# A two-layer state-space and mixture-of-experts kernel: gate products dealt out one a slot, and the first layer's blocks taken out a slot later

## The chip, the core and the metric

The kernel runs on one core of a Trainium2 chip. The core has a matrix engine (PE, with its weight loads listed as PEld), a vector engine (DVE), an activation engine (ACT), a general engine (POOL) and a queue processor for transfers (SP). Each runs its own list of instructions in order; they wait for each other through semaphores. The metric is the device time of one execution in microseconds (us). Before the change the median of three executions is 685.33 us (684.86 to 688.0).

## The reference

Two layers, each of the form x + s(norm(x)) * silu(f(norm(x))), on 8 sequences of 256 tokens with 128 features. s is a state-space scan, f a mixture of experts. Cut to what matters here:

```python
# layer 0, experts: one expert per token
h = relu(einsum('te,td,edf->tf', onehot, xn, W1) + b1[idx])
y = (einsum('te,tf,efd->td', onehot, h, W2) + b2[idx]) * gates
# layer 1, experts: all 8 experts for every token, F = 512
g = einsum('bsh,ehf->ebsf', x, w_gate)
u = einsum('bsh,ehf->ebsf', x, w_up)
h = silu(g) * u
expert_out = einsum('ebsf,efh->ebsh', h, w_down)
out = einsum('ebsh,bse->bsh', expert_out, cw)
# both layers, scan over tokens, 16 states per feature
s = s * exp(delta * A) + (delta * x) * B
y = sum over the states of s * C
```

## The kernel before, in words

The 2048 tokens are worked on in 4 pairs of sequences (PAIRS), 512 tokens at a time, so that most tiles are 128 x 512. The program of every engine is written as a walk over slots: 32 slots (UNITS) to a pair, 128 in the first layer and 128 in the second. Tables of slot numbers say what an engine does in which slot, and the text of a slot function says in which order. There is no planner: the numbers are written by hand. A slot is an order and no time; an engine goes on as soon as the semaphores let it.

**The scan** is cut into chunks, one for each state index. In the first layer there are 16 chunks to a pair, one every two slots (CH0), in the second 32, one a slot but for one slot with two (CHUNKS1). For each chunk ACT forms the decay (exp), DVE forms the drive (L899 in the first layer, L922 in the second) and runs the scan (L907, L929), and POOL multiplies the state by C (L1320 or L1324, in the second layer L1275) and adds it to a running sum (L1326, L1277). There are 4 state buffers (RING), so DVE can be at most 4 chunks ahead of POOL; and 6 decay buffers (SIX).

**First layer, experts.** The tokens are sorted by expert into 15 blocks of 256 rows. Block b goes through these steps, whose slots hang on UP_AT (20, 24, ... 64, then 67, 70, 73): POOL starts the load of the expert's weights (load_pack, an indirect DMA, L1226) five slots before; PE transposes the rows (turn_block, two slots before); ACT copies them (turn_in, L1613); PE forms the hidden layer (up_block, L1815); ACT applies relu (L1621); PE multiplies by W2 (down_block, L1827, three slots after); DVE adds the bias and takes the result out of PSUM (take_out, L1005, at TAKE_AT, five slots after); SP stores it (eight slots after). The weights have three buffers, so load_pack(b) waits for the take of block b - 3. In the same slots DVE also forms wl, the low part of the second layer's gate weights (split_low, L743), two operands in SBUF.

**Second layer, experts.** 8 experts with 4 tiles of the hidden layer each make 32 units to a pair, one a slot. Unit u takes: the gate product on PE (gate1, three passes in three instructions, L1911 to L1913, into one of two PSUM banks, HIDS = 2), Silu on ACT (L1676, into one of six buffers sg), the up product on PE (up1, L2023, in slot u + 1), the multiplication of the two on DVE (finish_hidden, L1059, in slot u + 2), and the down product on PE (down1, L2041, in slot u + 3). Within a slot PE does its gate products first, then down1, then up1, then the heads of the next pair. ACT runs the 4 Silus of an expert in one burst, since exp and Silu need different tables, and behind them the decays of the chunks that are scanned 3 to 6 slots later. With experts 3 to 6 a head of the next pair ("xi0", "xi1", "z0", "z1" in EXTRA) goes through the same two banks between two experts. POOL also weighs the tokens of expert e + 1 (weigh_tokens, L1384), after the last up product of expert e - 1.

The gate products before: with units 4e to 4e + 3 of expert e, PE does two (one, where EXTRA has a head) in slot 4e - 1, and the other two or three in slot 4e.

Of the kernel before, what the change touches and what calls it, by code (L numbers as in the profile page):

```python
# [37 lines left out]
E, FT = 8, 4  # L38
UNITS = E * FT
# [42 lines left out]


EXTRA = {3: "xi0", 4: "xi1", 5: "z0", 6: "z1"}
PE1 = {6: "xnT", 8: "logits", 9: "xi0a", 10: "xi0b", 13: "row0 xi1a", 15: "cwT xi1b", 17: "dt0", 18: "z0",
       20: "row1", 22: "dt1 z1"}
ACT1 = {5: "xn", 7: "xnT", 10: "lexp", 14: "row0", 15: "cwT", 19: "dt0", 21: "row1", 23: "dt1", 26: "ln", 29: "hand xr",
# [40 lines left out]
SCATTER_AT = [k // 4 for k in range(NT)]  # L128
UP_AT = [20 + 4 * b if b < 12 else 31 + 3 * b for b in range(BLOCKS)]
TURN_AT, TURN_IN_AT = [at - 2 for at in UP_AT], [at - 1 for at in UP_AT]  # L130
RELU_AT, DOWN_AT, TAKE_AT = ([at + lag for at in UP_AT] for lag in (1, 3, 5))
PACK_AT, LOAD_AT = ([at + lag for at in UP_AT] for lag in (-5, -5))
STORE_AT = [at + (8 if b < BLOCKS - 2 else 6) for b, at in enumerate(UP_AT)]
ROWS_AT = 18
# [49 lines left out]
def now(slots, u):  # L184

    if isinstance(slots, dict):
        return slots.get(u, "").split()
    return [c for c, at in enumerate(slots) if at == u]
# [28 lines left out]

STREAM = [item for e in range(E) for item in ([EXTRA[e]] if e in EXTRA else []) + list(range(FT * e, FT * e + FT))]
assert len(STREAM) % HIDS == 0


def stream_bank(item):

    return HID_BANK + STREAM.index(item) % HIDS


def stream_before(item, extras):

    items = [k for k in STREAM if extras or isinstance(k, int)]
    at, bank = STREAM.index(item), stream_bank(item)  # L230
    earlier = [k for k in items if stream_bank(k) == bank and STREAM.index(k) < at]
    return earlier[-1] if earlier else None
# [67 lines left out]
def build(nc, x, out, x1, crow, cwrow, sorted_in, sorted_out, w):  # L300
    ctx = ExitStack()
    with ctx:
# [209 lines left out]
        def use1(signal, j, step):  # L512
            return signal.sem, signal.at1(j, bank_order(j).index(step) + 1)
# [17 lines left out]
        def first_pair(j):  # L531

            return isinstance(j, int) and j == 0
# [915 lines left out]
        def _(act):  # L1449
# [132 lines left out]
            def keep(i):  # L1582

                act.wait_ge(*use1(head_read, i, "xi1"))
                act.wait_ge(s_ps.sem, s_ps.at1(i, 0))
                for m in range(J1):
                    a.activation(xd[:, m, :], xs[:, m, :], ACT.Identity, scale=col1("dskip", m))
                act.wait_ge(*use1(head_read, i, "z1"))
                act.wait_ge(yz_ready.sem, yz_ready.at1(i, 0))
                a.activation(szm[:, :, :], sz[:, :, :], ACT.Copy, scale=0.5).then_inc(kept_ready.sem, 1)  # L1590
# [15 lines left out]
            def form_decay(i, c):  # L1606
                exponential(in1(i), c, c // N, negA1, freed(c, i))
# [64 lines left out]
            def silu(i, u):  # L1672
                act.wait_ge(hid_ps.sem, hid_ps.at1(i, u + 1))

                act.wait_ge(hid_ready.sem, hid_ready.at1(i, freed(u, i)))
                a.activation(sg[:, PLACE[u], :], bank[stream_bank(u)][:, :], ACT.Silu).then_inc(silu_ready.sem, 1)  # L1676

            def slot1(i, u, head=None, j=None, late=None):
                e = u // FT
                if u == 0 and late is first_late:  # L1680
                    act.wait_ge(g_ready.sem, g_ready.at0(PAIRS, 0))
                if u == 0 and late:
                    late(u)
                if u % FT == 0:
                    if e in EXTRA and i + 1 < PAIRS:
                        head1({"x": "xs", "z": "sz"}[EXTRA[e][0]] + EXTRA[e][-1], i + 1)
                    for f in range(FT):
                        silu(i, u + f)
                    if u > 0 and late:
                        late(u)  # L1690
                    for c in DECAYS1[e]:
                        form_decay(i, c)
                elif late:
                    late(u)
                if u == (LATE if i else FIRST_LATE):
                    keep(i)
                if i + 1 < PAIRS:
                    for name in now(ACT1, u):
                        head1(name, i + 1)
# [40 lines left out]
            for u in range(FIRST_LATE):  # L1740
                slot1(0, u, late=first_late)
            for i in range(PAIRS - 1):
                for u in range(LATE if i else FIRST_LATE, UNITS):
                    slot1(i, u, head1, i + 1)
                for u in range(LATE):
                    slot1(i + 1, u, late=lambda u: late1(i, u))
# [7 lines left out]
        def _(pe):  # L1754
# [75 lines left out]
            def head_free(j, name):  # L1830

                order = bank_order(j)
                earlier = order[:order.index(name)]
                if first_pair(j):
                    same = [k for k in earlier if BANK_OF10[k] == BANK_OF10[name]]
                else:
                    same = [k for k in earlier if k not in EXTRA.values()]
                pe.wait_ge(head_read.sem, head_read.at1(j, order.index(same[-1]) + 1 if same else 0))

            def extra_free(j, name):  # L1840

                if first_pair(j):
                    head_free(j, name)
                    if BANK_OF10[name] == OUT_BANK:
                        pe.wait_ge(blk_out_ready.sem, blk_out_ready.at0(0, BLOCKS))
                    return
                before = stream_before(name, True)
                pe.wait_ge(silu_ready.sem, silu_ready.at1(j - 1, before + 1))
# [11 lines left out]
            def head1(name, j):  # L1860
# [3 lines left out]
                if name in ("xi0", "xi1", "xi0a", "xi1a", "z0", "z1"):  # L1864
                    extra_free(j, item)
                elif item not in EXTRA.values():
                    head_free(j, name)
# [41 lines left out]
            def three_passes(dst, e, f, stop):  # L1909
                ws = slice(128 * f, 128 * f + 128)  # L1910
                t.matmul(dst, wh[:, e, ws], XH[:, :], start=True, stop=False)  # L1911
                t.matmul(dst, wh[:, e, ws], XL[:, :], start=False, stop=False)  # L1912
                return t.matmul(dst, wl[:, e, ws], XH[:, :], start=False, stop=stop)  # L1913
# [30 lines left out]
            def gate1(i, u):  # L1944
                e, f = u // FT, u % FT
                if u == 0:
                    pe.wait_ge(xl_ready.sem, xl_ready.at1(i, 1))
                    if first_pair(i):
                        pe.wait_ge(*use1(head_read, 0, "cwT"))
                if f == 0:  # L1950
                    pe.wait_ge(wl_ready.sem, wl_ready.at0(0, e + 1))

                before = stream_before(u, i + 1 < PAIRS)
                if before is None:
                    pe.wait_ge(silu_ready.sem, silu_ready.at1(i, u + 1 - HIDS))
                elif isinstance(before, int):
                    pe.wait_ge(silu_ready.sem, silu_ready.at1(i, before + 1))
                else:
                    pe.wait_ge(*use1(head_read, i + 1, before))
                three_passes(bank[stream_bank(u)][:, :], e, f, True).then_inc(hid_ps.sem, 1)  # L1960
# [83 lines left out]
            def slot1(i, u, head=None, j=None, late=None):  # L2044
                if u == 0 and late:
                    late(u)
                more = i + 1 < PAIRS
                if u % FT == 0:
                    for k in range(1 if more and u // FT in EXTRA else 2, FT):
                        gate1(i, u + k)  # L2050
                if u % FT == FT - 1 and u + 1 < UNITS:
                    for k in range(1 if more and (u + 1) // FT in EXTRA else 2):
                        gate1(i, u + 1 + k)
                if u > LAG1:
                    down1(i, u - LAG1)
                if u > 0 and late and u <= LAG1:
                    late(u)
                if u == LAG1:
                    down1(i, u - LAG1)
                if u > 0:  # L2060
                    up1(i, u - 1)
                if late and u > LAG1:
                    late(u)
                if u == UNITS - 1 and more:
                    gate1(i + 1, 0)
                    gate1(i + 1, 1)
                if i + 1 < PAIRS:
                    for name in now(PE1, u):
                        head1(name, i + 1)
                else:  # L2070
                    for n in now(LAST_SUM_AT, u):
                        sum_last(n)
# [38 lines left out]
            for u in range(FIRST_LATE):  # L2111
                slot1(0, u, late=lambda u: late0(PAIRS - 1, u))
# [88 lines left out]
```

## Time and profile before

| what | value |
|---|---|
| median of three executions | 685.33 us |
| the profiled execution, its own time | 684.94 us |
| its span, first to last instruction | 683.2 us |
| DVE busy | 585.9 us (86%) |
| PE busy | 576.1 us (84%) |
| POOL busy | 533.4 us (78%) |
| ACT busy | 451.9 us (66%) |
| mean granted clock of PE | 0.962 |
| first scan of the first layer starts | 41.0 us |
| first scan of the second layer starts | 255.5 us |
| last scan starts | 667.9 us |

Busy time is what the records of an engine cover; matmuls are pipelined and their ends modelled, so starts are the better measure on PE. "Idle before" is how long an engine stood still ahead of an instruction, and the name behind the arrow is what it was waiting for. Lines of matmuls with x2 are one fp32 product recorded in two parts. The 1.7 us between the span and the time lie around the first and the last instruction.

### The profile page before, as it was taken

The numbers are of one execution on the slowest core, as the hardware profiler recorded it, in microseconds if no ns is written. First come the engines' busy times: TensorE is split into PE (matmuls) and PEld (weight loads), VectorE is DVE, ScalarE is ACT, GpSimd is POOL, SyncE is SP. The second block draws the span as 40 slices with busy tenths as digits, with TensorE's granted clock in tenths as the row PEclk, the third lists the DMA queues.
The fourth block names the chain that finished last, engine by engine and source line by source line (L and its number), as shares of the span: only waits on it lengthen the run. The fifth ranks groups of instructions, "written<-read, shape, count | busy, mean of one in ns | idle before, by whom it ended". The sixth has DMA issues, their size and how long they took to land. (4 is left out here: it accounts for less than half of the span.)

```text
span 683.2 us, 8361 instructions
## 1 busy us (share of the span) xinstructions
PE 576.1 (84%) x2075; PEld 331.4 (49%) x2075; DVE 585.9 (86%) x921; ACT 451.9 (66%) x708; POOL 533.4 (78%) x431
## 2 busy tenths in 40 slices
PE   3646998889638957999999799999799999799997
PEld 2411676667214423644444454444354444566674
DVE  6899887879898979997879988988989788898995
ACT  4555676866724768757786766787665887766660
POOL 3456568665884577987998899999799999799991
PEclk9998999999877989999999999999999999999999
DMA  8087988997888677776667678657676867787970
GB/s 264 23 309 229 321 315 260 305 342 234 269 266 282 200 175 182 193 199 164 168 165 204 169 192 209 184 158 201 170 198 181 214 164 184 182 213 202 231 190 17
DMA packets 71216, 142.25 MB, mean 208 GB/s; under 512 B 8352, under 2 KB 37088, under 8 KB 71168
## 3 DMA queue, kind: packets, MB, share of 16 engines
q1 hardware_dynamic: 67984, 130.74, 68.1%
q0 software_dynamic: 3184, 10.98, 4.7%
q8 instruction: 17, 0.28, 0.2%
q14 instruction: 31, 0.25, 0.1%
HBM read 133.23 MB, written 8.45 MB: 207 GB/s over the span
## 5 line engine op out<-in xcount | busy, mean ns | idle before, releaser
L929 DVE TENSOR_TENSOR_SCAN state<-decay,bank 128x512 f32<-128x512 f32 x128 | 155.9, 1218 | 13.4 <-POOL product L1275 5.4
L2023 PE MATMUL bank<-xw,wu 128*128 128x512 f32 x256 | 133.0, 601 | 13.7 <-DVE hid L1059 13.5
L1275 POOL TENSOR_TENSOR product<-state,CB 128x512 f32<-128x512 f32 x90 | 116.8, 1297 | 17.7 <-DVE state L929 13.9
L1277 POOL TENSOR_TENSOR product<-product 128x512 f32<-128x512 f32 x90 | 119.8, 1332 | 7.1
L1676 ACT ACTIVATE sg<-bank 128x512 f32<-128x512 f32 x128 | 75.4, 597 | 65.7 <-PE bank L1913 56.9
L2041 PE MATMUL bank<-hid,wd 128*128 128x512 f32 x192 | 99.1, 597 | 6.0 <-DVE hid L1059 6.0
L1059 DVE TENSOR_TENSOR hid<-sg,bank 128x512 f32<-128x512 f32 x128 | 84.9, 665 | 21.8 <-PE bank L2023 20.2
L1925 PE MATMUL bank<-product,early 128*128 128x512 f32 x112 | 71.7, 739 | 33.6 <-POOL product L1320 14.6
L922 DVE TENSOR_TENSOR bank<-bank,CB 128x512 f32<-128x512 f32 x128 | 88.8, 694 | 12.8 <-DMA CB<-crow 10.9
L1596 ACT ACTIVATE decay<-delta,negA 128x510 f32<-128x510 f32 x128 | 82.5, 710 | 10.7 <-DVE delta L887 5.4
L1911 PE MATMUL bank<-XH,wh 128*128 128x512 f32 x128 | 73.5, 574 | 10.5 <-ACT sg L1676 3.7
L907 DVE TENSOR_TENSOR_SCAN state<-decay,bank 128x512 f32<-128x512 f32 x64 | 77.9, 1216 | 2.8
L2023 PEld LDWEIGHTS bank<-xw,wu 128*128 128x128 f32 x256 | 45.4, 191 | 63.7 <-issue 46.5
L1320 POOL TENSOR_TENSOR product<-state,CB 128x512 f32<-128x512 f32 x31 | 40.5, 1305 | 23.6 <-DVE state L907 16.6
L1604 ACT ACTIVATE decay<-delta,negA 128x510 f32<-128x510 f32 x64 | 44.9, 714 | 16.5 <-DVE state L907 16.3
L1925 PEld LDWEIGHTS bank<-product,early 128*128 128x128 f32 x112 | 22.4, 229 | 64.5 <-POOL product L1320 27.4
L2041 PEld LDWEIGHTS bank<-hid,wd 128*128 128x128 f32 x192 | 35.1, 189 | 34.5 <-issue 25.9
L1913 PE MATMUL bank<-XH,wl 128*128 128x512 f32 x128 | 50.6, 395 | 0.0
L1912 PE MATMUL bank<-XL,wh 128*128 128x512 f32 x128 | 50.5, 395 | 0.0
L1911 PEld LDWEIGHTS bank<-XH,wh 128*128 128x128 f32 x128 | 24.4, 190 | 39.3 <-ACT sg L1676 13.3
L1596 ACT ACT_TABLE_LOAD x32 | 41.1, 1283 | 0.6
L1384 POOL TENSOR_TENSOR xw<-XR,cwb 128x512 f32<-128x512 f32 x30 | 39.4, 1312 | 2.4 <-PE bank L2023 1.0
(240 smaller groups left out, 1117.7 us busy)
## 6 DMA issues: line engine op xcount, KB each, us to landing
CB<-crow SPq DMA_DIRECT2D x256, 256.0 KB, 4.1
CB<-crow SPq DMA_DIRECT2D x44, 512.0 KB, 5.0
cwb<-cwrow SPq DMA_DIRECT2D x32, 256.0 KB, 4.6
szm<-crow SPq DMA_DIRECT2D x11, 512.0 KB, 5.3
cwb<-crow SPq DMA_DIRECT2D x9, 512.0 KB, 5.6
xw<-Wg_dram SPq DMA_DIRECT2D x8, 256.0 KB, 4.5
wd<-Wd_dram SPq DMA_DIRECT2D x8, 256.0 KB, 5.7
wu<-Wu_dram SPq DMA_DIRECT2D x8, 256.0 KB, 4.7
```

Of the source, the lines that this page charges most:

```text
L907: v.tensor_tensor_scan(state[:, g % RING, :], place0(g), drive, 0.0, ALU.mult, ALU.add).then_inc(state_ready.sem, 1)
L922: v.tensor_tensor(drive, dx, CB[:, c % ROWS, 1, :], ALU.mult).then_inc(drive_ready.sem, 1)
L929: v.tensor_tensor_scan(state[:, c % RING, :], decay[:, PLACE[c], :], drive, 0.0, ALU.mult, ALU.add).then_inc(state_ready.sem, 1)
L1059: v.tensor_tensor(hid[:, u % 2, :], sg[:, PLACE[u], :], bank[up_bank(i, u)][:, :], ALU.mult).then_inc(hid_ready.sem, 1)
L1275: p.tensor_tensor(addend, state[:, c % RING, :], cs, ALU.mult).then_inc(state_used.sem, 1)
L1277: ins = p.tensor_tensor(product[:, m, :], product[:, m, :], addend, ALU.add)
L1596: a.activation(by_batch(decay[:, PLACE[c], :])[:, :, 1:], by_batch(delta[:, m, :])[:, :, 1:], ACT.Exp, scale=negA[:, c:c + 1]).then_inc(de ...
L1676: a.activation(sg[:, PLACE[u], :], bank[stream_bank(u)][:, :], ACT.Silu).then_inc(silu_ready.sem, 1)
L1911: t.matmul(dst, wh[:, e, ws], XH[:, :], start=True, stop=False)
L1925: t.matmul(bank[Y_BANK][:, :], ident[:, :], product[:, PRODUCT_OF[n], :], start=(c == 0), stop=(group[-1] % N == N - 1)).then_inc(summed.s ...
L2023: t.matmul(bank[up_bank(i, u)][:, :], wu[:, e, 128 * f:128 * f + 128], xw[:, e % 2, :], start=True, stop=True).then_inc(up_ps.sem, 1)
L2041: ins = t.matmul(bank[OUT_BANK][:, :], wd[:, u, :], hid[:, u % 2, :], start=(u == 0), stop=(u == UNITS - 1))
```

## The change

Three edits. (1) The order of the gate products in the second layer comes from two tables instead of the two if-statements. In pairs with a next pair (GATE1_AT): expert 0 as before but for unit 3 in slot 1 (nothing lies between there); expert 1 as before (3, 3, 4, 4); experts 2 and 7 one a slot (6 to 9, and 26 to 29); experts 3 to 6 in slots 4e - 1, 4e, 4e, 4e + 1. In the last pair (GATE1_LAST) every expert but 1 has one a slot. (2) ACT's Silus of an expert other than 1 are written as two in slot 4e and two in slot 4e + 1, with the decays behind the second two. (3) take_out of blocks 0 to 10 stands six slots after up_block instead of five.

```diff
+GATE1_LAST = [-1, -1] + [k // FT * FT + (-1, -1, 0, 0)[k % FT] if k // FT == 1 else k - 2 for k in range(2, UNITS)]
+GATE1_AT = [k // FT * FT + (-1, 0, 0, 1)[k % FT] if k // FT in EXTRA else at for k, at in enumerate(GATE1_LAST)]
...
-RELU_AT, DOWN_AT, TAKE_AT = ([at + lag for at in UP_AT] for lag in (1, 3, 5))
+RELU_AT, DOWN_AT = ([at + lag for at in UP_AT] for lag in (1, 3))
+TAKE_AT = [at + (6 if b < 11 else 5) for b, at in enumerate(UP_AT)]
...
-                    for f in range(FT):
+                    for f in range(FT if e == 1 else 2):
                         silu(i, u + f)
                     if u > 0 and late:
                         late(u)
+                elif u % FT == 1 and e != 1:
+                    for f in range(2):
+                        silu(i, u + 1 + f)
+                    if late:
+                        late(u)
+                elif late:
+                    late(u)
+                if u % FT == (0 if e == 1 else 1):
                     for c in DECAYS1[e]:
                         form_decay(i, c)
-                elif late:
-                    late(u)
...
-                if u % FT == 0:
-                    for k in range(1 if more and u // FT in EXTRA else 2, FT):
-                        gate1(i, u + k)
-                if u % FT == FT - 1 and u + 1 < UNITS:
-                    for k in range(1 if more and (u + 1) // FT in EXTRA else 2):
-                        gate1(i, u + 1 + k)
+                for k in now(GATE1_AT if more else GATE1_LAST, u):
+                    gate1(i, k)
```

PE, first pair of the second layer, slots 16 and 17 (expert 4, units 17 to 19). L1911 to L1913 are one gate product (L1920 to L1922 after, the lines having moved by nine), `hid,wd` is down1, `xw,wu` is up1. Before:

```order
L1911 MATMUL bank2<-XH,wh 128x512
L1912 MATMUL bank2<-XL,wh 128x512
L1913 MATMUL bank2<-XH,wl 128x512
L1911 MATMUL bank3<-XH,wh 128x512
L1912 MATMUL bank3<-XL,wh 128x512
L1913 MATMUL bank3<-XH,wl 128x512
L2041 MATMUL bank1<-hid,wd 128x512
L2023 MATMUL bank5<-xw,wu 128x512
L2041 MATMUL bank1<-hid,wd 128x512
L2023 MATMUL bank0<-xw,wu 128x512
```

After:

```order
L1920 MATMUL bank2<-XH,wh 128x512
L1921 MATMUL bank2<-XL,wh 128x512
L1922 MATMUL bank2<-XH,wl 128x512
L2050 MATMUL bank1<-hid,wd 128x512
L2032 MATMUL bank5<-xw,wu 128x512
L1920 MATMUL bank3<-XH,wh 128x512
L1921 MATMUL bank3<-XL,wh 128x512
L1922 MATMUL bank3<-XH,wl 128x512
L2050 MATMUL bank1<-hid,wd 128x512
L2032 MATMUL bank0<-xw,wu 128x512
```

The gate product of unit 19 has moved from ahead of slot 16's down and up product to behind them. The same happens with the fourth unit of experts 2 to 7 in every pair; with experts 2 and 7 (in the last pair with experts 2 to 7) the first unit also moves a slot ahead.

DVE, first layer, block 8, slots 57 and 58. `hid<-bank1,wd` is take_out, `bank4<-bank6` the drive of a chunk, `state<-decay,bank4` its scan, `wl<-xw,wh` split_low. Before:

```order
L899 TENSOR_TENSOR bank4<-bank6,cwb 128x512
L907 SCALAR_TENSOR_TENSOR state<-decay,bank4 128x512
L1005 TENSOR_TENSOR hid<-bank1,wd 128x256
L899 TENSOR_TENSOR bank4<-bank6,szm 128x512
L743 TENSOR_TENSOR wl<-xw,wh 128x512
L907 SCALAR_TENSOR_TENSOR state<-decay,bank4 128x512
```

After:

```order
L902 TENSOR_TENSOR bank4<-bank6,cwb 128x512
L910 SCALAR_TENSOR_TENSOR state<-decay,bank4 128x512
L902 TENSOR_TENSOR bank4<-bank6,szm 128x512
L1008 TENSOR_TENSOR hid<-bank1,wd 128x256
L746 TENSOR_TENSOR wl<-xw,wh 128x512
L910 SCALAR_TENSOR_TENSOR state<-decay,bank4 128x512
```

The take of the block now comes behind the next chunk's drive instead of ahead of it. With blocks 3, 4, 6 and 7 it also passes one or two operations of a head.

On ACT, POOL and SP every row is the same before and after: in slots 4e of all experts but the second there is nothing that ACT does between the second and the third Silu, so writing the burst in two halves changes no order.

## Rows read from the trace of the kernel before

**Rows 1.** stretches: start:end, length, busy PE, PEld, DVE, ACT, POOL, clock, DMA, GB/s.
```profile
85.00:170.00 85.00, 76.56 (x410) 58.55 (x409) 69.54 (x106) 59.87 (x120) 56.29 (x46) 0.96 0.86 292
295.00:325.00 30.00, 29.05 (x83) 14.25 (x81) 25.23 (x36) 20.62 (x30) 24.32 (x20) 1.00 0.69 180
365.00:390.00 25.00, 20.43 (x75) 11.48 (x74) 22.73 (x37) 20.02 (x30) 20.80 (x18) 1.00 0.67 170
```

**Rows 2.** waits of POOL, 255 to 683 us: total us, times, longest us.
```profile
POOL product L1275 <- DVE state L929: 13.9, 12, 2.2
```

**Rows 3.** timeline of POOL, second layer: start, us, engine, line, operation, idle before.
```profile
314.07 1.29 POOL L1275 TENSOR_TENSOR product<-state,CB 128x512 f32<-128x512 f32 x1 [0.94 <-DVE state L929]
...
317.73 1.30 POOL L1384 TENSOR_TENSOR xw<-XR,cwb 128x512 f32<-128x512 f32 x1 [1.02 <-PE bank L2023]
320.28 1.28 POOL L1275 TENSOR_TENSOR product<-state,CB 128x512 f32<-128x512 f32 x1 [1.25 <-DVE state L929]
...
383.19 1.28 POOL L1275 TENSOR_TENSOR product<-state,CB 128x512 f32<-128x512 f32 x1 [1.90 <-DVE state L929]
...
427.67 1.28 POOL L1275 TENSOR_TENSOR product<-state,CB 128x512 f32<-128x512 f32 x1 [0.34 <-DVE state L929]
```

**Rows 4.** timeline of DVE, first pair of the second layer, slots 17 to 19.
```profile
317.59 0.69 DVE L1059 TENSOR_TENSOR hid<-sg,bank 128x512 f32<-128x512 f32 x1 [3.60 <-PE bank L2023]
...
318.98 1.22 DVE L929 TENSOR_TENSOR_SCAN state<-decay,bank 128x512 f32<-128x512 f32 x1
...
321.48 1.22 DVE L929 TENSOR_TENSOR_SCAN state<-decay,bank 128x512 f32<-128x512 f32 x1
```

**Rows 5.** timeline of PE, the same stretch, its slot 16.
```profile
314.47 0.40 PE L1913 MATMUL bank<-XH,wl 128*128 128x512 f32 x1
314.87 0.50 PE L1911 MATMUL bank<-XH,wh 128*128 128x512 f32 x1
...
315.67 1.02 PE L2041 MATMUL bank<-hid,wd 128*128 128x512 f32 x2
316.53 1.02 PE L2023 MATMUL bank<-xw,wu 128*128 128x512 f32 x2
```

**Rows 6.** timeline of ACT, the same expert: its last Silu and its decays.
```profile
315.87 0.60 ACT L1676 ACTIVATE sg<-bank 128x512 f32<-128x512 f32 x1 [0.37 <-PE bank L1913]
...
317.78 2.55 ACT L1596 ACTIVATE decay<-delta,negA 128x510 f32<-128x510 f32 x4
```

**Rows 7.** waits of DVE in the first layer, 40 to 250 us.
```profile
DVE hid L1005 <- PE bank L1827: 12.5, 8, 3.6
```

**Rows 8.** timeline of DVE in the first layer.
```profile
93.93 0.75 DVE L846 SCALAR_TENSOR_TENSOR sp_e<-xpad,early,sp_e 128x512 f32<-128x512 f32 x1 [1.17 <-ACT sp_e L1481]
...
119.03 0.42 DVE L1005 TENSOR_TENSOR hid<-bank,wd 128x256 f32<-128x256 f32 x1 [3.64 <-PE bank L1827]
...
119.98 0.69 DVE L899 TENSOR_TENSOR bank<-bank,CB 128x512 f32<-128x512 f32 x1
120.58 1.38 DVE L743 TENSOR_TENSOR wl<-xw,wh 128x512 fp32r<-128x512 f32 x1
...
132.73 0.42 DVE L1005 TENSOR_TENSOR hid<-bank,wd 128x256 f32<-128x256 f32 x1 [2.53 <-PE bank L1827]
```

**Rows 9.** timeline of PE in the first layer.
```profile
86.61 1.95 PE L1827 MATMUL bank<-wd,sg 128*128 128x128 f32 x16
88.73 1.96 PE L1815 MATMUL bank<-sg,wd 128*128 128x256 f32 x8 [0.18 <-issue]
...
126.14 3.29 PE L1815 MATMUL bank<-sg,wd 128*128 128x256 f32 x8 [2.44 <-ACT sg L1613]
...
138.32 1.96 PE L1815 MATMUL bank<-sg,wd 128*128 128x256 f32 x8 [0.91 <-issue]
```

**Rows 10.** DMA issues by tensor: count and median us to landing.
```profile
wd<-pack_dram,rows_of POOLq DMA_INDIRECT x15, 7.0
```

**Rows 11.** the line that forms wl: ns min/median/max of one, first and last start.
```profile
L743 DVE TENSOR_TENSOR wl<-xw,wh x8: 678/681/1379, 89.5 to 186.6; 128x512 fp32r<-128x512 f32 x8
```

## The prediction

> **What bounds the kernel now.** I read the busy times by stretch first, then the waits of POOL and DVE, and then the timelines where these waits lie.
>
> In the first layer's block stretch (85 to 170 us) PE is busy 76.6 of 85 us and DVE 69.5, at a granted clock of 0.96 [rows 1]. Neither runs through: DVE hands states to POOL, POOL issues the weights of a block, PE multiplies, DVE takes the block out. The reader is to see a ring of engines here, and a wait in it tells nothing until one knows what the engine behind it was waiting for.
>
> In the second layer the engine to watch is POOL. Of its idle time 13.9 us, in 12 waits, are waits for a scan ahead of L1275 [rows 2]. The timeline says where: in the first pair (0.94, 1.02 and 1.25 us), a single 0.34 us in the second, and at the start of every pair, as the 1.90 us at 383.19 [rows 3]. The last kind lies where DVE is busy 22.7 of 25 us (third of [rows 1]): DVE is late there by its own work, and no edit touches that. Nearly everywhere else POOL runs without a gap, and a DVE that comes earlier only fills the four state buffers.
>
> **The second layer, part by part.** No product is added or removed; three gate products per expert move. What matters is what they stand ahead of. In slot 16 of the first pair DVE stands 3.60 us for the up product of unit 15, the longest wait of that layer [rows 4], because PE does three gate products before it. The third begins when its predecessor ends (314.47 + 0.40 = 314.87) and the down product behind it starts at 315.67, so it takes 0.80 us [rows 5]. Behind the up product, it frees that product 0.80 us earlier. DVE's multiplication goes from 317.59 to 316.8, the scan of 318.98 to 318.2, and POOL's weighing of 317.73, which waited for the same product, to 316.9. POOL's next product, at 320.28, follows the scan, also 0.80 earlier. So 1.02 + 1.25 us of idle time fall by 0.80 and not to nothing, for PE is busy 29.05 of 30 us here (second of [rows 1]): it has as much to do as before, and what leaves slot 16 stands ahead of the next up product. Bounds: 0 if that next product takes it all back, 2.27 if both waits go. I take 0.80.
>
> In the second pair the same wait of DVE costs POOL 0.34 (last of [rows 3]): I take it whole, from 0 to 0.34. In the third and fourth pair expert 4 leaves no gap on POOL: 0. In experts 5 to 7 of all pairs DVE waits less or not for PE and POOL is busy throughout: 0; the cover is POOL's queue of states, and if it were gone a moved gate would be worth its 0.80 there too. The gate of unit 8, which moves ahead into slot 6, falls in the part where DVE is the late one and PE waits for it: 0. Sum for the second layer: 0.80 + 0.34 = 1.14 us.
>
> ACT's Silus in two halves: its order does not change, so no table load and no operation is added, 0. What changes is the wait of the last Silu for a gate that comes later. Before, it starts at 315.87 and the decays at 317.78, 0.64 each (2.55 for four) [rows 6]; the first of them is used by the scan of slot 19, at 321.48 [rows 4], which leaves 321.48 - 318.42 = 3.06 us. The gate now comes behind a down and an up product, whose starts lie 0.86 apart [rows 5], so 1.72 later, and the scan comes 0.80 earlier: 0.54 us remain. Hidden, narrowly, by DVE's own operations between two scans. If the cover is gone the scan waits for its decay: the first rival on the slow side.
>
> **The first layer.** take_out of blocks 0 to 10 moves behind the next drive. DVE waits 12.5 us in 8 places for PE's down product at this line [rows 7], two of them 3.64 and 2.53 us [rows 8]. The drive, which starts 0.60 us before its follower (119.98 to 120.58) [rows 8], now runs inside the wait. So where DVE waits it gets ahead by 0.60 us, once. It can't be added up over the blocks if PE doesn't come earlier: the next take then waits longer by the same 0.60. Is PE itself waiting for DVE? Three cases show in its rows. Early, PE is back to back: the down product of 86.61 lasts to 88.56 and the up product starts at 88.73, with 0.18 idle [rows 9]; the block before it has the same picture. In the middle the up product of 126.14 waited 2.44 us for ACT [rows 9], whose queue DVE's take doesn't reach; the lead is lost there. Late, 0.91 us before 138.32 [rows 9], named "issue". PE waits for no engine there, and the weights of that block come by a DMA that needs 7.0 us to land [rows 10]; POOL issues it behind the product of a state which DVE delivers. That one comes earlier when DVE is earlier. I count the two early ones with 0.18 each, 0.36, rounded up to 0.4 for DVE's next wait, for ACT at 93.93 (1.17 us) [rows 8], which goes back to PE as well; and the late one with the 0.60 of the lead, as the next load is tied to the scan and not to the gap. Sum 1.0 us. Bounds: 0, if ACT's chain at 126 us and the loads eat all; 4.2, if each of six waiting takes gives back 0.60 and the one at 119.03 a further 0.60 for the head's operation it also passes. I take 1.0, since the rows of PE speak for a ring with little slack.
>
> For blocks that did not wait the take is the same 0.42 us [rows 8] a step later: 0. POOL's load of block b + 3 waits for the take. It stands behind the product of a state that DVE scans in the same stretch, so it is ready as before except for blocks 12 and 13, whose loads wait one DVE step more (0.42 + 0.69); POOL has only work behind it that needs the scan after that. The store on SP has two slots left instead of three: 0.
>
> One place where the Trainium skill speaks against the edit. split_low (wl) takes 0.68 us as a rule and 1.38 once, at 120.58 [rows 8, 11]. The page "SBUF — State Buffer", section "Who interferes with whom", says that a DVE instruction with two SBUF inputs and a GpSimd instruction that reads SBUF shut each other out for a whole instruction. The trace agrees with that one row of eight. By that rule, moved steps may meet POOL's operations anew, and the sum would shrink.
>
> Sum: 1.14 + 1.0 = 2.14 us. The profiled execution took 684.94 us, 0.39 less than the median 685.33; from the median the forecast is 683.2, and I give 683.1 for the small waits of PE for Silus, which the dealing out removes and which I did not count.
>
> **The rivals.**
> A. The first layer keeps every removed wait: 4.2 instead of 1.0, in all 5.3 us, 680.0. For it: the waits are real idle time of a DVE that is busy 82% there. Against: PE at 90% in the same stretch and the wait for ACT at 126.14.
> B. The second layer's first pair loses all of POOL's idle time around expert 4: 0.94 + 1.02 + 1.25 + 0.34 = 3.55, with the first layer's 1.0 in all 4.55 us, 680.8. For it: PE's order is smoother in every slot, and DVE's shorter waits at 307 to 312 us may help too. Against: PE's 97% there.
> C. Slower: the decays come late. Its place is the scan in slot 4e + 3 of experts 2 to 7, it decides from 0.54 us of further delay of the last Silu. Were half of the 24 places uncovered and late by 0.5 us each, that is 6 us against 2.1 gained: 689.2. For it: 0.54 is little, and ACT has a table load before the decays. Against: the Silu waits for the same PE whose up product DVE needs as well, so the two are late together.
> D. DVE's moved steps meet POOL: three more of wl's kind of collision, 0.70 each (1.38 - 0.68), take 2.1 us back: 685.2. For it: the row at 120.58. Against: it can as well remove that one.
>
> **How the numbers follow.** Forecast 0.40, A 0.22, B 0.14, C 0.10, D 0.14. A measurement of this kernel tells about 0.5% (3.4 us) from no change. Faster by more: A, B and 0.05 of the forecast, 0.41. Within: 0.35 of the forecast and 0.13 of D, 0.48. Slower: C and 0.01 of D, 0.11. The range takes in A, B, D and the near side of C: 679.0 to 686.8. The likeliest case's own range is 681.0 to 684.9.
>
> **What would show it.** In the profile after, around 317 us: DVE's wait for the up product shrinks from 3.60 by 0.8 (A says the same, B by 2 and more), and POOL's 1.02 nearly goes. The first scan of the second layer, at 255.5 us before, starts near 254.5; at 251.3 A is right. DVE's waits at L1005 fall from 12.5 to 9 us or less, without the layer getting shorter by as much. Decays before L929 show no wait for ACT; if they do in many places, C. The last scan, at 667.9, should start near 665.8. The forecast is wrong if the layers' two parts don't come to 1 us each, above all if PE's gaps ahead of L1815 stay and the first layer is still shorter.

## The result, and the profile after

Slower. The median is 691.0 us (685.1 to 696.17, 20 runs) against 686.07 (683.38 to 688.0, 20 runs) for the kernel before in the same measurement. The ratio is 1.0071, with a 95% interval of 1.0046 to 1.0096. The forecast was 683.1 us and the range ended at 686.8.

The profiled execution has a span of 690.3 us, 7.1 more than before. It took 692.09 us, 1.1 more than the median, so the profiles show a larger difference than the 4.9 us between the medians. Where it went is read from the starts of the scans: the first scan of the second layer (chunk 0) starts at 255.59 us, before at 255.46, where I had forecast 254.5. So the first layer is even in these two profiles. From there to the last scan it takes 419.5 us (675.08 - 255.59), before 412.5 (667.93 - 255.46). Nearly all of the 7.1 us lie in the second layer, where I had forecast 1.14 us of gain.

The stretches of [rows 1], after (start:end, length, busy PE, PEld, DVE, ACT, POOL, clock, DMA, GB/s):

```profile
85.00:170.00 85.00, 76.95 (x413) 59.76 (x412) 69.60 (x103) 60.97 (x122) 54.80 (x45) 0.96 0.87 290
295.00:325.00 30.00, 28.89 (x82) 14.20 (x80) 26.23 (x37) 20.02 (x29) 25.44 (x21) 1.00 0.70 186
365.00:390.00 25.00, 21.95 (x78) 12.33 (x77) 23.62 (x39) 19.66 (x30) 20.59 (x17) 1.00 0.61 160
```

None of them shows the loss: the stretches I had chosen are not those where it happens. The waits do, for the second layer (total us, times, longest). First POOL's, then PE's, then DVE's:

```profile
POOL product L1278 <- DVE state L932: 23.0, 15, 2.9
```

```profile
PE bank L1920 <- ACT sg L1679: 7.4, 6, 2.3
PE bank L1773 <- ACT rows L1565: 5.1, 3, 1.7
```

```profile
DVE hid L1062 <- PE bank L2032: 31.7, 18, 4.5
```

POOL's wait for scans grew from 13.9 us [rows 2] to 23.0. DVE's wait for up products grew from 20.2 to 31.7. And PE now waits for ACT: 5.1 us for a copy named `rows`, a wait that the kernel before does not have in this layer, and 7.4 us for Silus, before 1.7. The reader should see a chain here, which the experiments below test: ACT late, hence PE, hence DVE, hence POOL.

**At expert 4 the step went as forecast at first.** The mixed timeline of the kernel after around 316 us (start, us, engine, line, operation, idle before):

```profile
315.17 1.02 PE L2032 MATMUL bank<-xw,wu 128*128 128x512 f32 x2
315.63 0.80 PE L1920 MATMUL bank<-XH,wh 128*128 128x512 f32 x1
...
316.23 0.69 DVE L1062 TENSOR_TENSOR hid<-sg,bank 128x512 f32<-128x512 f32 x1 [2.36 <-PE bank L2032]
...
316.65 1.30 POOL L1387 TENSOR_TENSOR xw<-XR,cwb 128x512 f32<-128x512 f32 x1
...
316.73 1.02 PE L2050 MATMUL bank<-hid,wd 128*128 128x512 f32 x2
...
317.61 1.22 DVE L932 TENSOR_TENSOR_SCAN state<-decay,bank 128x512 f32<-128x512 f32 x1
...
318.91 1.28 POOL L1278 TENSOR_TENSOR product<-state,CB 128x512 f32<-128x512 f32 x1 [0.96 <-DVE state L932]
```

DVE's 3.60 us [rows 4] are 2.36, the scan has moved from 318.98 to 317.61, and POOL's 1.02 [rows 3] is gone. The gain is 1.25 us (the scan before this one was 0.12 us ahead already). But the scan of chunk 22 starts at 331.82, before at 331.78: the lead is gone within one expert, and before PE stands still for anything that is told below. 0.41 us of it went in one DVE operation of the next pair's head (L859, 1.45 us at 330.45, before 1.04 at 330.81), the rest by longer waits for PE's up products.

The page of the profile puts a mean of 676 ns on L1920, before 574 on L1911, as if a gate product cost more between other products. The starts say otherwise. From the up product at 315.17 to the down product at 316.73 it is 1.56 us; 0.86 of it is the distance of two such products, and 0.70 is left for the gate product between them, where the kernel before spends 0.80.

**At expert 5 the loss begins.** Before, around 333 us:

```profile
327.89 0.60 ACT L1676 ACTIVATE sg<-bank 128x512 f32<-128x512 f32 x1 [0.36 <-PE bank L1913]
328.51 1.28 ACT L1596 ACT_TABLE_LOAD   x1
...
329.80 2.55 ACT L1596 ACTIVATE decay<-delta,negA 128x510 f32<-128x510 f32 x4
...
332.26 0.58 ACT L1562 ACTIVATE rows<-bank 96x512 f32<-96x512 f32 x1
...
333.79 1.12 PE L1764 MATMUL bank<-rows,w_dt 32*128 32x512 f32 x2
...
334.95 0.69 ACT L1488 ACTIVATE sp_e<-bank,early 128x512 f32<-128x512 f32 x1 [2.11 <-PE bank L1764]
...
337.37 1.02 PE L2023 MATMUL bank<-xw,wu 128*128 128x512 f32 x2
...
338.42 0.69 DVE L1059 TENSOR_TENSOR hid<-sg,bank 128x512 f32<-128x512 f32 x1 [0.44 <-PE bank L2023]
```

After, the same place:

```profile
330.80 0.60 ACT L1679 ACTIVATE sg<-bank 128x512 f32<-128x512 f32 x1 [2.68 <-PE bank L1922]
331.42 1.28 ACT L1599 ACT_TABLE_LOAD   x1
...
332.71 2.55 ACT L1599 ACTIVATE decay<-delta,negA 128x510 f32<-128x510 f32 x4
...
335.17 0.57 ACT L1565 ACTIVATE rows<-bank 96x512 f32<-96x512 f32 x1
...
335.89 1.09 PE L1773 MATMUL bank<-rows,w_dt 32*128 32x512 f32 x2 [1.69 <-ACT rows L1565]
...
339.11 1.91 PE L2050 MATMUL bank<-hid,wd 128*128 128x512 f32 x2
...
340.82 1.28 PE L2032 MATMUL bank<-xw,wu 128*128 128x512 f32 x2
...
342.13 0.69 DVE L1062 TENSOR_TENSOR hid<-sg,bank 128x512 f32<-128x512 f32 x1 [4.11 <-PE bank L2032]
...
345.28 1.27 POOL L1278 TENSOR_TENSOR product<-state,CB 128x512 f32<-128x512 f32 x1 [2.93 <-DVE state L932]
```

The last Silu of the expert is 2.91 us later, since its gate product (unit 23) stands behind a down product, an up product and a product of the next pair's head. Behind that Silu ACT has a table load, four decays and the copy `row1` (`rows`). The decays are in time: no scan waits for one. The copy is not: PE's queue has the product dt1 next, and stands still for 1.69 us. The stretches 335:339, 339:342 and 342:345, before:

```profile
335.00:339.00 4.00, 3.38 (x9) 1.46 (x9) 3.47 (x5) 3.91 (x6) 3.84 (x4) 1.00 0.94 242
339.00:342.00 3.00, 2.49 (x10) 1.76 (x11) 2.44 (x4) 2.14 (x4) 2.84 (x3) 1.00 0.47 139
342.00:345.00 3.00, 3.00 (x9) 1.32 (x8) 1.13 (x2) 2.81 (x4) 2.84 (x3) 1.00 0.54 152
```

and after:

```profile
335.00:339.00 4.00, 3.11 (x7) 1.71 (x8) 2.93 (x4) 2.66 (x6) 3.84 (x4) 0.86 0.39 98
339.00:342.00 3.00, 3.00 (x6) 1.27 (x6) 0.00 (x0) 2.97 (x4) 2.84 (x3) 0.61 0.86 232
342.00:345.00 3.00, 3.00 (x12) 1.82 (x10) 2.87 (x4) 1.20 (x3) 0.35 (x1) 1.00 1.06 243
```

After the standstill the granted clock falls: its mean over 339 to 342 us is 0.61, near the lower of the two levels (1.2 of 2.4 GHz), and the down product takes 1.91 us instead of 1.02. PE is busy 3.00 of 3 us there, and DVE 0.00: a full row of PE is a slow PE. DVE's multiplication is 3.71 us late (342.13 against 338.42, from scans that were even). Of it 2.10 is dt1 (335.89 against 333.79), and 1.61 the rest of the way (1.35 until the up product starts, 0.26 its own length).

Not all of the 3.71 us stay. The scan behind that multiplication (chunk 25) is 3.71 us late too, the next one (chunk 26) only 1.36 (346.62 against 345.26), because the kernel before waits 2.43 us for its next up product there and this one does not wait. In the second and third pair 1.66 and 1.71 us stay at this place. That is 4.7 us of the 7.0 in all; the runs below price this one gate product at 3.9 and 5.5 us.

**At the change from expert 6 to 7** there is a second one. After:

```profile
352.78 1.28 ACT L1679 ACT_TABLE_LOAD   x1
...
354.08 1.09 ACT L1679 ACTIVATE sg<-bank 128x512 f32<-128x512 f32 x2
...
354.73 0.61 PE L1920 MATMUL bank<-XH,wh 128*128 128x512 f32 x1 [2.28 <-ACT sg L1679]
...
355.99 1.91 PE L2050 MATMUL bank<-hid,wd 128*128 128x512 f32 x2
...
359.10 0.69 DVE L1062 TENSOR_TENSOR hid<-sg,bank 128x512 f32<-128x512 f32 x1 [3.77 <-PE bank L2032]
```

Unit 27's gate is late, so expert 6's decays, the head's `ln` with its table loads, and the first Silu of expert 7 are late, and PE waits 2.28 us for the PSUM bank that this Silu frees; before it waited 0.58. From chunk 29 to the first chunk of the next pair 1.43, 0.31 and 0.34 us are added in the three pairs, 2.1 us in all; the first is the pair whose granted clock falls behind the wait:

```profile
355.00:359.00 4.00, 4.00 (x8) 1.98 (x8) 0.33 (x1) 0.76 (x2) 3.76 (x4) 0.58 0.78 204
```

In the first layer DVE's waits at the take fell, as the prediction wanted, from 12.5 us [rows 7] to 7.3. The profile of `warm_dt1` below, with the same first layer, has 10.5, so one profile says little here.

### The profile page after: what moved, and what is told of

Same layout as the page of the kernel before. It is cut to its first block and busy times, and to the rows that moved or that the text cites. A ratio compares the mean times of both kernels' runs of the same rounds, so it can differ in the third digit from the quotient of the medians.

```text
span 690.3 us, 8361 instructions
## 1 busy us (share of the span) xinstructions
PE 579.1 (84%) x2075; PEld 335.9 (49%) x2075; DVE 588.7 (85%) x921; ACT 450.6 (65%) x708; POOL 531.9 (77%) x431
## 5 line engine op out<-in xcount | busy, mean ns | idle before, releaser
L1062 DVE TENSOR_TENSOR hid<-sg,bank 128x512 f32<-128x512 f32 x128 | 85.2, 667 | 33.8 <-PE bank L2032 31.7
L2050 PE MATMUL bank<-hid,wd 128*128 128x512 f32 x192 | 101.2, 609 | 2.8 <-DVE hid L1062 2.8
L1920 PE MATMUL bank<-XH,wh 128*128 128x512 f32 x128 | 86.6, 676 | 16.0 <-ACT sg L1679 9.3
L1922 PE MATMUL bank<-XH,wl 128*128 128x512 f32 x128 | 51.7, 404 | 0.0
L1920 PEld LDWEIGHTS bank<-XH,wh 128*128 128x128 f32 x128 | 24.8, 194 | 49.2 <-issue 17.9
```

Source lines behind the costliest of these rows:

```text
L1062: v.tensor_tensor(hid[:, u % 2, :], sg[:, PLACE[u], :], bank[up_bank(i, u)][:, :], ALU.mult).then_inc(hid_ready.sem, 1)
L2050: ins = t.matmul(bank[OUT_BANK][:, :], wd[:, u, :], hid[:, u % 2, :], start=(u == 0), stop=(u == UNITS - 1))
```

## The experiments

Ratios are to the kernel before on the same chip, each with its 95% interval. "Unit 23 back" means that its gate product stands in slot 20 again, "unit 27 back" in slot 24, in the first three pairs.

**1. The two halves of the change apart.** `take_only`: the kernel before with

```diff
-RELU_AT, DOWN_AT, TAKE_AT = ([at + lag for at in UP_AT] for lag in (1, 3, 5))
+RELU_AT, DOWN_AT = ([at + lag for at in UP_AT] for lag in (1, 3))
+TAKE_AT = [at + (6 if b < 11 else 5) for b, at in enumerate(UP_AT)]
```

> Only take_out of blocks 0 to 10 a slot later, the second layer as before. Theory H (ACT hands over late: the loss is all in the second layer): the first scan of the second layer starts within 0.3 us of 255.5 us and the time is that of before, ratio 0.999 to 1.001. Rival T (the take's move costs, for down_block b + 1 now waits for it behind a head's operation, 1.99 us at 108.5 in the changed kernel's trace): second layer later by 0.5 us or more, ratio above 1.001. My prediction had it 1.0 us earlier, ratio 0.9985.

0.9988 (0.9961 to 1.0015). In its profile the first scan of the second layer starts at 252.53 us, 2.9 earlier than before, which neither H nor T had; part 6 shows how far such starts spread. `gates_only` is the changed kernel with these lines as before.

> Only the gate products dealt out (and the Silus written in two halves), take_out as before. H: the whole loss is here, ratio 1.006 to 1.010, PE waits for ACT's copy of rows ahead of dt1 three times, 1.7 us each, and for ACT's Silu ahead of unit 30's gate, 2.3 us each. T: ratio clearly below the changed kernel's, under 1.004.

1.0104 (1.0060 to 1.0148), with PE's waits for `rows` of 5.1 us and for sg of 7.4, as in the changed kernel. That is just above H's 1.010, with a wide interval. The loss belongs to the gates.

**2. Single gates put back.** `u23_back` is the changed kernel with

```diff
+GATE1_AT[23] = 20
```

> The changed kernel with the gate product of unit 23 (expert 5's fourth) back in slot 20. H: ACT's Silu, decays and copy of rows come 2.7 us earlier, so PE's 5.1 us of waits for rows vanish and the granted clock around 340 us stays at 1.0; the waits ahead of unit 30's gate stay. Time 2 to 4 us under the changed kernel, ratio to before 1.001 to 1.005. Rival O (dealt-out gates cost PE more each, by the changes of weights between them): the time falls by a seventh of the loss only, 1 us.

0.9990 (0.9967 to 1.0014): 0.0081 under the changed kernel, some 5.5 us for three gate products, more than the 2 to 4 us that I expected. The waits for `rows` are gone, the clock of 335 to 345 us is 1.00. `u23_u27_back` has `GATE1_AT[27] = 24` besides:

> Units 23 and 27 (the fourth of experts 5 and 6) back in slots 20 and 24. H: both kinds of PE waits for ACT vanish, what stays is the gain at expert 4: ratio to before 0.996 to 0.999. Rival O: ratio still above 1.003, since 6 of 8 moved gates per pair are still dealt out.

0.9964 (0.9938 to 0.9990), PE's waits for sg down from 7.4 us to 2.3. `u27_back` has unit 27 back alone:

> The changed kernel, with unit 27's gate product (expert 6) back in slot 24; unit 23's stays dealt out. With the kernel that has 23 back (0.999 of before) and the one that has both (0.9964) this completes the square. If the two places add up: 27 is worth 0.0026, so this comes to 1.0045, 2 us under the changed kernel; PE's waits for sg fall from 7.4 to 2.3 us, those for rows stay at 5.1. If instead expert 6's loss is what is left of expert 5's (one is late because the other is), 27 alone is worth nothing: 1.007.

1.0041 (1.0021 to 1.0061), sg 2.3 and `rows` 5.1 us. So the square is additive: unit 23 costs 0.0081 with 27 dealt out and 0.0077 without, unit 27 costs 0.0030 and 0.0026 (the latter two are about as large as their uncertainty, but PE's waits tell the same). `u19_back_too` has units 19, 23 and 27 back:

> The changed kernel with units 19, 23 and 27 back in slots 16, 20 and 24 of the first three pairs: of the dealing out only experts 2 and 7 and the last pair are left, and the takes of the first layer. Beside the kernel that has 23 and 27 back (0.9964) it tells what expert 4's move is worth. If my step for expert 4 was right (DVE's wait of 3.60 at 317 falls by about 0.8 and lasts to the end of the pair once experts 5 and 6 don't lose it): 1 to 2 us slower than that kernel, 0.998 to 1.0. If the lead is lost again at expert 5 whatever is done there: the same as that kernel, 0.996 to 0.997, and the gain comes from the first layer and experts 2 and 7.

0.9983 (0.9962 to 1.0005), against 0.9964 with unit 19 dealt out. The difference, 0.0019 or 1.3 us, is within what the expectation gave the step for expert 4, and the second layer is 412.9 us against 411.7 in the two profiles; but the intervals overlap, so it is not shown.

**3. Unit 23 alone**, in the kernel before:

```diff
-                        gate1(i, u + k)
+                        if not (more and u + k == 23):
+                            gate1(i, u + k)
+                if more and u == 21:
+                    gate1(i, 23)
```

> The kernel before, with one thing changed: unit 23's gate product stands in slot 21 in place of 20, in the first three pairs. Nothing else is dealt out and the first layer is as before. Theory Q (this one move, through ACT's queue, makes most of the loss): the changed kernel with 23 put back was 0.0081 of the time under the changed kernel, so this one comes out as much over the one before: 1.006 to 1.009, PE's wait for ACT rows three times, about 5 us, DVE's wait ahead of the scan of chunk 27 about 4 us each time. If the loss needs the others (late Silus that add up along experts 4 to 6): under 1.004.

1.0057 (1.0037 to 1.0076). Its waits, PE's and then DVE's of the first pair:

```profile
PE bank L1764 <- ACT rows L1562: 5.1, 3, 1.7
```

```profile
341.77 0.69 DVE L1059 TENSOR_TENSOR hid<-sg,bank 128x512 f32<-128x512 f32 x1 [4.51 <-PE bank L2023]
```

One gate product moved by one slot, three times, makes 3.9 us of the 4.9 us. It is a little under what I expected (1.006 to 1.009); the interval takes in both. DVE's wait is 4.5 us in each of the three pairs, ahead of the scan of chunk 25 (the "chunk 27" of the expectation counts two scans of the token sorting with the chunks).

**4. Is it the Silu, or the queue behind it?** `row1_early` is the changed kernel with the copy ahead of the decays; unit 23 stays dealt out.

```diff
+                if u == 21 and i + 1 < PAIRS:
+                    head1("row1", i + 1)
                 if u % FT == (0 if e == 1 else 1):
                     for c in DECAYS1[e]:
                         form_decay(i, c)
...
                     for name in now(ACT1, u):
-                        head1(name, i + 1)
+                        if name != "row1":
+                            head1(name, i + 1)
```

> The changed kernel, with one ACT operation moved: the copy of the next pair's rows (row1) is written ahead of the four decays of expert 5, not behind them; unit 23's gate product stays behind slot 20's down and up product. Theory Q (the late Silu itself costs nothing, ACT's queue behind it does: PE stands 1.7 us per pair ahead of dt1, and its granted clock falls behind that): PE's waits 'L1773 <- ACT rows' (3 times, 5.1 us) go to under 1 us, the granted clock of 335 to 342 us is 0.95 or more instead of 0.61 to 0.86, the second layer gets shorter by 3 to 5 us, time 0.995 of the changed kernel's, 1.001 to 1.004 of the one before. Theory G (a dealt-out gate product costs PE by its place between down and up products, with more weight changes): no change, 1.007, and the gate passes of that stretch stay at 0.6 us.

0.9990 (0.9969 to 1.0010), the same as with unit 23 back and less than the 1.001 to 1.004 expected:

```profile
329.65 0.60 ACT L1679 ACTIVATE sg<-bank 128x512 f32<-128x512 f32 x1 [2.68 <-PE bank L1925]
330.14 0.58 ACT L1565 ACTIVATE rows<-bank 96x512 f32<-96x512 f32 x1
...
332.98 1.12 PE L1776 MATMUL bank<-rows,w_dt 32*128 32x512 f32 x2
...
337.61 0.69 DVE L1062 TENSOR_TENSOR hid<-sg,bank 128x512 f32<-128x512 f32 x1 [0.76 <-PE bank L2035]
```

The Silu waits for PE as long as in the changed kernel (2.68 us), and it costs nothing that these runs can tell. The copy comes 0.49 us behind it and PE doesn't stop. The control is the kernel before with only the copy moved:

> Control: the kernel before, all its gate products in their places, with only ACT's copy row1 of the first three pairs moved ahead of the four decays of expert 5. If row1_early got its 5.4 us back because the late copy was the way in which unit 23's gate hurt, then here, where PE never waits for the copy, there is little to win: 0.998 to 1.002. If the earlier copy is a gain of its own (an earlier load of CB): 0.992 to 0.995, and then row1_early says nothing of unit 23.

1.0002 (0.9985 to 1.0020). An early copy is worth nothing measurable by itself, only where the gate is late. Theory G falls with this pair of runs: the gate product stands where it stood, and the loss is gone.

**5. Standstill or clock?** `warm_dt1` is the changed kernel with PE kept at work during the standstill:

```diff
+                        if name == "dt1":
+                            extra_free(i + 1, "z1")
+                            for _ in range(2):
+                                t.matmul(by_batch(extra_bank(i + 1, "z1")), w_in1[:, 0:128], XNT, start=True, stop=True)
                         head1(name, i + 1)
```

> The changed kernel, with two throwaway fp32 products of 128x512 on PE ahead of dt1 in the first three pairs, 0.86 us each by the starts of such products: as long as the wait of 1.69 us that stands there. Nothing is done earlier; PE only doesn't stand still. Theory W (the larger part of the loss is the lowered clock behind the standstill): the granted clock of 335 to 342 us stays at 0.95 or more, the down product behind takes 1.02 instead of 1.91 us and the gate passes 0.4 instead of 0.6, 1 to 1.5 us a pair back, in all 3 to 4 us, 1.002 to 1.003 of the kernel before. Theory S (the standstill itself is the loss, the clock a bystander): same time as the changed kernel, 1.007, or 0 to 1 us more.

1.0059 (1.0037 to 1.0081): not the 1.0025 of theory W. In the first pair:

```profile
335.69 1.88 PE L2077 MATMUL bank<-XNP,later 128*128 128x512 f32 x4
...
337.54 1.09 PE L1773 MATMUL bank<-rows,w_dt 32*128 32x512 f32 x2
...
340.22 1.02 PE L2050 MATMUL bank<-hid,wd 128*128 128x512 f32 x2
...
342.13 0.69 DVE L1062 TENSOR_TENSOR hid<-sg,bank 128x512 f32<-128x512 f32 x1 [2.47 <-PE bank L2032]
...
345.05 0.70 DVE L925 TENSOR_TENSOR bank<-bank,CB 128x512 f32<-128x512 f32 x1 [2.23 <-DMA CB<-crow]
```

On PE theory W holds: the granted clock of 335 to 345 us is 1.00, the down product takes 1.02, and DVE's wait is 1.64 us shorter, as the 1.61 above says. The end says something else. The next operation, the drive of chunk 25, waits 2.23 us for the load of CB. The data of this load have long been written; what is late is its issue. In SP's queue the program puts the write of `rows` to `crow` just ahead of the load of CB for chunk 25, so SP stands at that write until the late copy is there, and the loads behind it wait too. First this run, then the changed kernel:

```profile
337.42 0.79 SPq L599 DMA_DIRECT2D crow<-rows  x2
338.26 6.62 SPq L592 DMA_DIRECT2D CB<-crow  x8
```

```profile
335.77 0.79 SPq L599 DMA_DIRECT2D crow<-rows  x2
336.60 5.75 SPq L592 DMA_DIRECT2D CB<-crow  x8
```

SP's waits for this copy are 24.2 us in the second layer of the changed kernel, 8.0 at most, and before 11.5 and 3.7. In the changed kernel the late load was hidden behind the slow PE: its drive starts at 342.74 without a wait, 6.14 us behind the first of these loads. Here it starts 6.79 us behind it, so at least 0.65 of the 2.23 us are the load's own spread. In the other two pairs the wait is 0.25 and 0.74 us. Of the 1.6 us the scan of chunk 25 gets 0.5 in those two pairs, and in the first it is 0.7 us later than in the changed kernel. So the clock made the loss at PE longer, but the late copy also holds the pair up by a second way, and what remained of the gain is within the measurement. Theory S, in which the clock is a bystander, is right about the time and wrong about the mechanism.

**6. The first layer's price again, and both repairs.** `u23_u27_back_no_take` has units 23 and 27 back and the takes as before:

> The changed kernel with units 23 and 27 back in slots 20 and 24 and the first layer's takes back at five slots: the gate products of experts 2, 4, 7 and of the last pair alone. With takes at six slots it was 0.9964. It prices the edit of the first layer a third time (two pairs so far: 0.9988 against 1, and 1.0071 against 1.0104). If the takes bring the 1.0 us that I forecast: 0.998. If they bring nothing: 0.9964. If they bring the upper bound of 4.2 us: 1.0025.

0.9986 (0.9962 to 1.0010), against 0.9964 with the new takes. `row1_early_u27_back` has the early copy and unit 27 back:

> The changed kernel with both repairs: unit 27's gate back in slot 24, and the row1 copy ahead of the decays while unit 23 stays dealt out. If the two losses are separate and add up: 1.0071 - 0.0081 - 0.0030 = 0.996, as with both gates put back (0.9964), and PE waits neither for rows (0) nor for more than 2.5 us for sg. If mending one uncovers the other again: 0.999 or more.

0.9952 (0.9935 to 0.9969): 682.64 us (680.59 to 683.79, 9 runs) against 685.82 for the kernel before. The two repairs add up, and this version beats both kernels. Why it is better than before by 3.3 us is not settled by one profile: its second layer has 412.8 us there, the kernel before 412.5, and between profiles of the same code such a length differs by about 1 us (413.3 in `take_only`). In these two profiles the difference lies ahead of the second layer, whose first scan starts at 252.83 us against 255.46.

## Why the prediction was wrong

The step that failed is the price of ACT's late Silus, which the sum put at nothing; it turned a small gain into a loss. The gain at expert 4 also did not last as it was forecast.

- **"ACT's Silus in two halves: 0, hidden, narrowly."** This failed, twice over. The delay was mis-sized: I let the gate pass a down and an up product (1.72 us), but in expert 5 the first product of the next pair's head stands there too, 2.91 us in the trace. And I asked only who uses the decays. They were covered. What wasn't is the next thing in ACT's queue, the copy `row1`, on which PE's own queue hangs and SP's too, with the loads of CB behind it. Its cover can be read in the kernel before: the copy ends at 332.84, and PE gets to dt1 at 333.70 (332.84 + 0.86 for the up product ahead), so 0.86 us. A delay of 2.91 us, less 0.86, less the 0.33 by which PE itself came later, is 1.72; the wait measured is 1.69. Even my own 1.72 us of delay would have overrun it. The 2.11 us that ACT waits at 334.95 in the kernel before look like room, but they lie behind the copy.
- **"In experts 5 to 7: 0; the cover is POOL's queue of states."** I asked what a gain is worth there, not what a loss is. The cover is there, but it is shorter than the loss: POOL's product of chunk 25 starts 1.03 us later than before (345.28, with a wait of 2.93, against 344.25) behind a scan that is 3.71 us late. (By the tables one gate product moves in each of experts 3 to 6 and two in experts 2 and 7, not three per expert as the prediction says; no term of the sum used the three.)
- **Expert 4, +0.80 and +0.34.** Direction and place right. The up product comes 1.36 us earlier (315.17 against 316.53); 0.40 of it PE was ahead at the first gate of the slot (312.82 against 313.22), 0.96 are the move, for which I had 0.80. What failed is that it should last: the lead was gone at chunk 22. The fault above did not take it, for PE stands still for the copy only from 334.20 on, and with units 23 and 27 back the first pair is no longer ahead at that scan either (19.36 us from chunk 17 to 22, before 19.02). In that profile it is 1.1 us ahead at the first chunk of the next pair, and what brings this is not shown; the ratios give expert 4's move about 1.3 us, not shown either. The 1.02 us of [rows 3] that I counted among POOL's waits for a scan is a wait for PE, as its row says.
- **First layer, +1.0.** About right, and better settled than one profile can: three pairs of kernels with and without the takes give 0.0012, 0.0033 and 0.0022, in the mean 0.0022 or 1.5 us. From the first scan of the first layer to the first of the second nine profiles with the new takes last 213.2 us in the mean and five with the old 214.1. Each of these is no larger than its uncertainty; together they speak for a gain of some 1 to 1.5 us and against the 4.2 of rival A. Single profiles spread from 211.2 to 216.8 us with the same code, so the even start of the second layer in the result tells nothing.
- **Rivals.** A and B fall. D, the meetings of DVE and POOL, does not make the loss: it goes when one ACT copy is moved, though the head's operation that takes 1.43 us instead of 1.04 stays in that run. C is nearest: it had the cause (the last Silu late) and its side, but its place was wrong. Its size (689.2 against a measured 691.0) is near by luck, for it was made of 12 places with 0.5 us each. It looked for scans that wait for decays, and there are none; DVE's waits are for PE. I gave it 0.10, with the argument that Silu and up product wait for the same PE and are late together. That left out that ACT's lateness goes back to PE.

Without the moves of units 23 and 27 the change is worth 0.0036 (`u23_u27_back`), 2.5 us, where the gains in the prediction summed to 2.14. The interval reaches from 0.7 to 4.3 us, and the gain of expert 4 did not run as forecast, so the sum is near without its terms being shown. What is shown is the missing cost.

## What to carry to other kernels

When an instruction is allowed to come later, go down the whole queue of the engine that waits for it, to the next instruction on which another engine's queue stands, not only to the results of its own kind. The cover is what the other engine still has to do ahead of such a hand-over (0.86 us here), however much idle time is listed elsewhere. One late operation can stop several queues: here the copy stopped PE's and SP's. And a late hand-over can often be mended where it is cheaper: here one copy moved ahead of four decays does what taking the gate back does.

## What the runs showed of the hardware

- A short standstill of PE is followed by a lowered clock, but not each time. Behind PE's 1.69 us for `rows` the mean granted clock of the next 6 us was 0.72 in all 12 cases of four profiles (the changed kernel, `gates_only`, `u23_alone`, `u27_back`). Behind the 2.28 us for sg, longer, it was 0.72 in 7 of 15 cases and 1.00 in 8, in five profiles of the same PE order around it; in the changed kernel in one pair of three. Behind nine waits of 1.12 to 1.47 us for sz (`u23_back`, `row1_early`, `warm_dt1`) and five of 1.52 to 1.58 us for xs it stayed at 1.00. So the length of the standstill alone does not decide; what does, stays open. Filling the gap with 1.88 us of throwaway products kept the clock at 1.00 in that place. The fall added 1.61 us to a dt1 that was 2.10 us late. A busy share does not show it: PE is busy 3.00 of 3 us at a granted clock of 0.61.
- A late load behind a slow engine is not seen until the engine is fast: CB's wait at one place went from nothing to 2.23 us when PE was kept at its full clock, of which at least 0.65 us is the spread of the load itself.
